# A four-layer graph network: message pass without bias matmuls, two gathered supers done last, sorted part ended earlier

## The reference, cut to what matters

```python
def _sage_mean(h, src, dst, Wl, Wr, b):
    agg = segment_sum(h[src], dst)          # over the edges
    cnt = segment_sum(ones, dst)
    return _l2norm(agg / maximum(cnt, 1) @ Wl + b + h @ Wr)
h = relu(batch_norm(_sage_mean(x, src, dst, Wl1, Wr1, b1)))   # 128 wide
out = _l2norm(_sage_mean(h, src, dst, Wl2, Wr2, b2) + x)      # 64 wide
x = _layernorm(x + out)
```

## Time and profile before

| | us |
|---|---|
| median of 3 runs | 8759.73 (8747.03 to 8762.27) |
| profiled execution, its own time | 8745.67 |
| its span, first to last instruction | 8743.7 |

### The profile page before, as it was taken

One profiled execution on the slowest core, in us unless ns is written; L12 is line 12 of the kernel. 1 busy time (PEld: TensorE's weight loads), 2 busy tenths in 40 slices (PEclk: granted clock), 3 DMA queues, 4 the chain that ended last, 5 costly groups with the idle time before them and its releaser, 6 DMA issues. The chain is left out here.

```text
span 8743.7 us, 127149 instructions
## 1 busy us (share of the span) xinstructions
PE 5411.1 (62%) x29370; PEld 4179.4 (48%) x29371; DVE 3367.5 (39%) x7842; ACT 1499.6 (17%) x3432; POOL 6302.1 (72%) x6643
## 2 busy tenths in 40 slices
PE   4456766666666666667788768778877333333333
PEld 3445555555666666655555545444444222222222
DVE  3224444434444444444445434555554111111111
ACT  1111111111111111112222212233333100000000
POOL 6777777767777777767777752777766477777777
PEclk6556556557777777767878865888888555555555
DMA  3111111113333333334545424544444111111111
GB/s 79 34 34 35 35 35 34 35 37 100 97 98 97 97 98 97 99 99 110 118 111 118 113 61 128 138 145 137 140 140 117 38 30 30 30 30 30 30 30 29
DMA packets 555851, 676.47 MB, mean 77 GB/s; under 512 B 242261, under 2 KB 358003, under 8 KB 555019
## 3 DMA queue, kind: packets, MB, share of 16 engines
q0 software_dynamic: 212448, 268.01, 15.6%
q1 hardware_dynamic: 201194, 306.89, 11.8%
q10 hardware_dynamic: 141441, 93.34, 3.5%
HBM read 574.09 MB, written 93.56 MB: 76 GB/s over the span
## 5 line engine op out<-in xcount | busy, mean ns | idle before, releaser
L1919 PE MATMUL PAG<-OH,G 128*64 128x96 f32 (+1 forms) x10224 | 1573.8, 337 | 2284.0 <-DMA G<-rel_tab,IDX 984.9
L1919 PEld LDWEIGHTS PAG<-OH,G 128*64 128x64 f32 (+1 forms) x10224 | 1424.7, 204 | 2438.6 <-issue 2415.3
L1919 PE MATMUL PH<-HT 125*128 125x192 bf16 (+4 forms) x10742 | 1991.2, 314 | 303.9 <-DVE HT L1449 92.2
L832 POOL DMA_INDIRECT G<-rel_tab,IDX x1507 | 1421.8, 943 | 546.3 <-issue 459.7
L832 POOL DMA_INDIRECT G<-in_x,SRC x1525 | 1451.6, 952 | 481.9 <-issue 464.6
L832 POOL DMA_INDIRECT G<-far_tab,SRC x1527 | 1442.3, 945 | 485.0 <-issue 465.2
L1919 PEld LDWEIGHTS PH<-HT 125*128 125x128 bf16 (+4 forms) x10742 | 1275.7, 156 | 995.6 <-issue 355.2
L1411 DVE TENSOR_TENSOR AGG<-AGG,PAG 64x96 f32 (+2 forms) x852 | 211.2, 248 | 3169.0 <-PE PAG L1919 3148.1
L832 POOL DMA_INDIRECT G<-g_tab,SRC x1040 | 991.6, 953 | 582.7 <-issue 498.5
L832 POOL DMA_INDIRECT G<-x_tab,SRC x1040 | 994.6, 956 | 334.7 <-issue 315.0
L1919 PE MATMUL PAG<-OH,HT 128*128 128x96 f32 x3126 | 611.0, 376 | 524.5 <-ACT HT L1127 518.0
(11 more groups left out here) (222 smaller groups left out, 4438.9 us busy)
## 6 DMA issues: line engine op xcount, KB each, us to landing
HT<-x_parts SPq DMA_DIRECT2D x160, 468.8 KB
HT<-g_parts SPq DMA_DIRECT2D x160, 468.8 KB
GROWS<-rel_tab SPq DMA_DIRECT2D x4096, 0.2 KB
GROWS<-in_x SPq DMA_DIRECT2D x3584, 0.2 KB
HT<-src_rows SPq DMA_DIRECT2D x320, 160.0 KB
rel_tab<-STG ACTq DMA_DIRECT2D x200, 250.0 KB
GROWS<-far_tab SPq DMA_DIRECT2D x3072, 0.5 KB
GROWS<-rel_tab ACTq DMA_DIRECT2D x3072, 0.2 KB
```

The lines of the kernel that those rows point to most:

```text
L832: pool.indirect_dma_start(out=G[:, h, j, 0:tabs[p].shape[1]], out_offset=None, in_=tabs[p], in_offset=bass.IndirectOffsetOnAxis(ap=numbers ...
L1919: return nc.tensor.matmul(dst, lhsT, rhs, start=start, stop=stop, skip_group_check=True)
```

## The change

Four edits.

1. **Message pass.** The two bias matmuls of a unit are gone. SP loads the bias once, spread over 125 partitions. ACT copies only the first half of the bank and stores it to `g_tab`; DVE adds the bias to the second half out of the bank into `MESSAGES`, and SP stores that to `r_tab`. PE's next unit waits for this addition.
2. **Held supers.** In layers 2 and 3 steps 28 and 29 work on the edges of supers 130 and 131, and steps 130 and 131 on those of 28 and 29 (`super_at`). Unit 7, to which 28 and 29 belong, comes last; unit 34 is free at step 30.
3. **Sorted part.** The batches are spread over steps 0 to 117 in place of 125. PE's last `sum_cells` stand before the sum of step 118, and DVE adds the last window at step 119.
4. **Places.** Layer 3 has four places a step, the fourth behind the second batch.

With this, DVE loads the window starts for two supers at a time, not four, and the check on the input has 9 limits in place of 5.

```diff
+HELD = 28
+HELD_UNIT = 7
+BEAT_SLOTS = {2: 3, 3: 4}
+def super_at(p, s):
+    if p not in CELL_LAYERS:
+        return s
+    early = SUPERS_OF[p] - 2
+    return {HELD: early, HELD + 1: early + 1, early: HELD, early + 1: HELD + 1}.get(s, s)
 def batches_by_step(p):
-        due = min(total, -(-total * (s + 1) // (supers - 6)))
+        due = min(total, -(-total * (s + 1) // (supers - 14)))
 def cell_schedule(p):
         if u < apart:
-            needs[u] = (min(at, supers), windows)
-            free[u] = at if at < supers else supers
+            if u < HELD_UNIT:
+                at = min(at, HELD)
+            elif u == HELD_UNIT:
+                at = supers
+            elif u == apart - 1:
+                at = HELD + 2
+            else:
+                at = min(at, supers - 2)
+            needs[u] = (at, windows)
+            free[u] = at
         else:
-            free[u] = step_of.get(BATCHES * windows, supers) + 1
+            free[u] = step_of.get(BATCHES * windows, LAST_BATCH_AT[p] + 2) + 1
-        for _ in range(3):
+        for _ in range(BEAT_SLOTS[p]):
# SP, messages()
+                sp.dma_start(BIAS[0:HALF, :], sb2.to_broadcast([HALF, D])).then_inc(bias_in, 16)
-                    sp.wait_ge(msg_copied, u + 1)
-                    sp.dma_start(rows_of(g_tab, u), MESSAGES[u % 2][0:HALF, :, 0:D]).then_inc(msg_out[u % 2], 16)
+                    sp.wait_ge(msg_rooted, u + 1)
+                    sp.dma_start(rows_of(r_tab, u), MESSAGES[u % 2][0:HALF, :, D:2 * D]).then_inc(msg_out[u % 2], 16)
# POOL: chunk numbers from t = super_at(p, s)
# ACT, messages()
-                    copy(rows_, MESSAGE_P[u % 2].rearrange("p (a c) -> p a c", a=2)).then_inc(msg_copied, 1)
+                    copy(rows_[:, :, 0:D], MESSAGE_P[u % 2].rearrange("p (a c) -> p a c", a=2)[:, :, 0:D])\
+                        .then_inc(msg_copied, 1)
-                    act.dma_start(rows_of(r_tab, u), rows_[:, :, D:2 * D]).then_inc(msg_out[u % 2], 16)
+                    act.dma_start(rows_of(g_tab, u), rows_[:, :, 0:D]).then_inc(msg_out[u % 2], 16)
# DVE, messages()
+                    if u >= 2:
+                        dve.wait_ge(msg_out[u % 2], 32 * (u // 2))
+                    nc.vector.tensor_tensor(MESSAGES[u % 2][0:HALF, :, D:2 * D],
+                                            MESSAGE_P[u % 2].rearrange("p (a c) -> p a c", a=2)[:, :, D:2 * D],
+                                            BIAS[0:HALF, :].unsqueeze(1).to_broadcast([HALF, 2, D]), ALU.add)\
+                      .then_inc(msg_rooted, 1)
# PE, messages()
-                        mm(bank[:, a * H:(a + 1) * H], POS[:, hot + a * HALF:hot + (a + 1) * HALF], wlr2[:, :], a == 0,
-                           False)
-                        last = mm(bank[:, a * H + D:(a + 1) * H], ONES[0:1, 0:HALF], sb2r, False, a == 1)
+                        last = mm(bank[:, a * H:(a + 1) * H], POS[:, hot + a * HALF:hot + (a + 1) * HALF], wlr2[:, :],
+                                  a == 0, a == 1)
# PE, cell_layer()
+                    if s == LAST_BATCH_AT[p] + 1:
+                        for e in range(pairs - LAG[p], pairs):
+                            sum_cells(e)
+                    for now in by_step[s][3:]:
+                        beats(now)
-                for e in range(pairs - LAG[p], pairs):
-                    sum_cells(e)
```

More of the change, by code:

```diff
@@ L60 @@
 IOTA_READY, SPANS_READY, DIAG_READY = 8, 22, 24
-ROWS_READY, COUNTED_READY, PREP_READY, TABLES_READY = 71, 85, 92, 100
+ROWS_READY, COUNTED_READY, PREP_READY, TABLES_READY = 80, 94, 101, 109
 ROWS_OUT = 5 * 16
@@ L94 @@
 CELL_LAYERS = {2: (132, 35), 3: (132, 35)}
+HELD = 28
+HELD_UNIT = 7
+assert HELD % 2 == 0 and SEGMENTS[0][0] <= HELD_UNIT < SEGMENTS[0][1]
 CELL_SUPERS = SLOTS
@@ L136 @@
 BATCHES_AT = {p: batches_by_step(p) for p in CELL_LAYERS}
+LAST_BATCH_AT = {p: max(s for s, batches in enumerate(at) if batches) for p, at in BATCHES_AT.items()}
 def cell_schedule(p):
@@ L283, in gnn_kernel @@
         REGULAR_I = sb("REGULAR_I", [1, 1], I32)
-        CHECKS = sb("CHECKS", [1, 2, 5])
+        CHECKS = sb("CHECKS", [1, 2, 9])
         DST_TAB = HT[:, N - SORTED * UNITS // 2:N].bitcast(F16).rearrange("p (w u) -> p w u", u=UNITS)
@@ L364, in gnn_kernel @@
         o += 2 * D
+        BIAS = HT[:, o:o + D]
+        o += D
         assert o <= N - SORTED * UNITS // 2
@@ L517, in gnn_kernel @@
         msg_split = sem("msg_split")
+        bias_in, msg_rooted = sem("bias_in"), sem("msg_rooted")
         msg_out = [sem("msg_out0"), sem("msg_out1")]
@@ L711, in some_rows @@
                     if at % AT_ONCE == 0:
-                        starts[:] = row_starts(sp, row_registers, p, SP_SUPERS[p][k] // 2, e)
+                        starts[:] = row_starts(sp, row_registers, p, super_at(p, SP_SUPERS[p][k]) // 2, e)
                     row(sp, p, k % ROW_BUFS, e, starts[at % AT_ONCE])
@@ L820, in _, with gathers @@
         def _(pool):
-            def gathers(p, s, base, by_rows=()):
+            def gathers(p, s, base, by_rows=(), edges_of=None):
                 numbers = IDX3 if p == 4 else SRC
@@ L828, in gathers @@
                     pool.wait_ge(summed, base + s + 1)
-                filled = GROUP - 1 if s in by_rows else filled_chunks(s)
+                t = s if edges_of is None else edges_of(p, s)
+                filled = GROUP - 1 if s in by_rows else filled_chunks(t)
                 for j in range(filled):
-                    c = s * GROUP + j
+                    c = t * GROUP + j
                     pool.indirect_dma_start(
@@ L835, in gathers, with layers @@
                     ).then_inc(gathered[h], 16 * (GROUP - j if j == filled - 1 else 1))
-            def layers(supers, base, rows):
+            def layers(supers, base, rows, edges_of=None):
                 for p in range(LAYERS):
@@ L848, in layers @@
                     for s in range(0 if p else SHARED, supers[p]):
-                        gathers(p, s, base[p], rows[p])
+                        gathers(p, s, base[p], rows[p], edges_of)
             even, even_base = [SUPERS] * LAYERS, [SUPERS * p for p in range(LAYERS)]
@@ L860, in _ @@
             with pool.If(regular > 0):
-                layers(SUPERS_OF, BASE, by_rows)
+                layers(SUPERS_OF, BASE, by_rows, super_at)
             with pool.If(regular < 1):
@@ L1284, in _ @@
             link(nc.vector.tensor_reduce(CHECKS[:, 0, 1:2], HT[0:1, 0:SORT_SUPERS], AX.X, ALU.max))
-            limits = [COLS - 1, 0] + [UNIT * apart - 1 for _, apart in CELL_LAYERS.values()] + [P]
+            limits = [COLS - 1, 0] + [UNIT * (apart - k) - WIN for _, apart in CELL_LAYERS.values() for k in (0, 1)]
+            limits += [UNIT * (HELD_UNIT + 1) - WIN, -UNIT * HELD_UNIT, P]
             for k, (supers, _) in enumerate(CELL_LAYERS.values()):
-                link(nc.vector.tensor_reduce(CHECKS[:, 0, 2 + k:3 + k], SPANS[0:1, 0:supers], AX.X, ALU.max))
+                link(nc.vector.tensor_reduce(CHECKS[:, 0, 2 + 2 * k:3 + 2 * k], FIRST[0:1, 0:supers], AX.X, ALU.max))
+                link(nc.vector.tensor_reduce(CHECKS[:, 0, 3 + 2 * k:4 + 2 * k], FIRST[0:1, 0:supers - 2], AX.X, ALU.max))
+            held = CHECKS[:, 0, 6:8]
+            link(nc.vector.tensor_reduce(held[:, 0:1], FIRST[0:1, HELD:HELD + 2], AX.X, ALU.max))
+            link(nc.vector.tensor_reduce(held[:, 1:2], FIRST[0:1, HELD:HELD + 2], AX.X, ALU.min))
+            link(nc.vector.tensor_scalar_mul(held[:, 1:2], held[:, 1:2], -1.0))
             for k, limit in enumerate(limits):
@@ L1729, in messages @@
             def messages():
+                dve.wait_ge(bias_in, 16)
                 for u in range(UNITS):
@@ L1840, in cell_layer @@
                 for s in range(supers):
-                    if s % SLOTS == 0:
-                        for k, w0 in enumerate(starts_of(dve, registers[s // SLOTS % 2], s)):
-                            starts[s + k] = w0
+                    if s % 2 == 0:
+                        pair = registers[s // SLOTS % 2][s % SLOTS:s % SLOTS + 2]
+                        starts[s], starts[s + 1] = starts_of(dve, pair, super_at(p, s))
                     if s:
@@ L1848, in cell_layer @@
                     if s + 1 < supers:
-                        one_hot((s + 1) % 2, DREL[:, s + 1, :]).then_inc(onehot_ready, 1)
+                        one_hot((s + 1) % 2, DREL[:, super_at(p, s + 1), :]).then_inc(onehot_ready, 1)
                     beats(by_step[s][0])
@@ L1856, in cell_layer @@
                         batch(g, s)
+                    for now in by_step[s][3:]:
+                        beats(now)
                     windows_before = max([0] + [g // BATCHES for at in BATCHES_AT[p][:s + 1] for g in at[-1:]])
-                if windows_before:
-                    dve.wait_ge(window_added, WINDOWS_BEFORE[p] + windows_before)
+                    if s == LAST_BATCH_AT[p] + 2:
+                        add_cells(p, windows - 1, s)
+                    if s >= LAST_BATCH_AT[p] + 2:
```

(3 more changed lines are left out.)

4 lines of the change are left out of this document (2 added, 2 removed).

## The result

The changed kernel takes 8783.44 us in the median (8778.69 to 8796.58), the kernel before 8759.73; the ratio is 1.0035 with a 95% interval of 1.0023 to 1.0046. By the medians it is slower by 24 us, by the ratio, which takes in all runs of both kernels, by some 31 us; I had forecast 10 us less. POOL's timeline says in which stage; rows as in the earlier trace rows.

What follows compares the result with a forecast made beforehand. POOL's gathers bound layer 2, PE's program layer 3, a `g_parts` store loop the message pass, with tails behind; −22 − 3 + 0.5 + 12 + 2 = −10.5 us gave 8749.2 us from the median, range 8708 to 8786.

Steps and rivals of the forecast that it cites:

- Tail of layer 2: Behind layer 2's last gather: 8 beats left instead of 17, two units instead of four; −22 us.
- Message pass: PE loses 200 matmuls, but the untouched store loop keeps 2.60 us a unit for 2.65; −3 us, bounds −54 and +10.
- the loop that I named: Message pass: DVE's split, SP's store, its landing, next split into that `g_parts` buffer; 5.20 us for two units.
- the estimate of 1.5 us a unit: Message pass: stores of 125 partitions on 5 engines, some 220 KB a unit, take at least 1.5 us.
- the −42: Message pass: most the bias edit would give, −42 us or less instead of −54, by the DMA engine rate.
- The three stretches: Layer 3: up to the sum of step 118 +40 us, then to the last gather −9, tail −30.5; together +0.5.
- the bound named there: Layer 3, sum of step 118 to last gather: if remaining units keep PE the bound, it stays 107.7 us (0).
- Four places a step: Layer 3: too little PE work between fold and flip, +8 us, denser `rel_tab` stores +4; +12, bounds −25 and +61.
- C: Layer 3: four places make PE wait for `XS` and `STG` in nearly every unit; +45 not +12, 8782 us; chance 0.22.
- B: Layer 3: PE's added work before step 118 fills waits for `GROWS`; +9 not +40, 8718 us; chance 0.33.
- D: Message pass follows PE because stores land sooner; −28 us instead of −3, 8724 us; chance 0.05.
- Prologue: Before the layers: nine more linked DVE instructions at 0.28 us; +2 us, between 0 and +2.5.

Runs made afterwards that it cites:

- l3_three_places: Changed kernel with three places a step in layer 3 instead of four, all else as changed; 8738.37 us, ratio 0.9979.
- l3_as_before: Changed kernel with layer 3 as before: three places, batches to step 125, supers in order; 8737.39 us, ratio 0.9982.
- l3_flip_5_later: Changed kernel, four places kept, one place left empty ahead of each unit's flip in layer 3; 8772.45 us, ratio 1.0023.

## Why the prediction was wrong

- *Tail of layer 2.* −22 predicted. The pass begins 5221.05 − 5190.2 = 30.8 us behind the last gather, it was 53.4: −22.6. Right.
- *Message pass.* −3 predicted; from its first matmul to the first gather of layer 3 137.45 us (5243.91 to 5381.36) became 132.9 (5221.05 to 5353.94), −4.6. The size was right, the cause wrong: the loop that I named does not hold the period, since it stayed at 2.59 us when that loop had four buffers and DVE's wait in it was gone; the transfers do, with the share of 5 of 16 engines never idle. That the size came right is luck: the loop's 5.20 us held a landing that the full transfers had stretched. The floor of 0.3 stands in the kernel before already. The Trainium skill's rule on the engines stood in the prediction as no more than an upper limit of the gain, and wrongly worked out: the estimate of 1.5 us a unit is below PE's own 1.58 and limits nothing, so the −42 does not follow from the numbers beside it.
- *Layer 3 without the places.* The three stretches +40 − 9 − 30.5 = +0.5. l3_three_places against l3_as_before is this part by itself: 1427.4 − 1396.1 = +31.3 in the stage (+31 predicted for the two first; singly, up to the end of the sum of step 118 1285.4 became 1323.8, +38.4 for +40, and behind it 110.7 became 103.6, −7.1 for −9), 53.7 − 89.7 = −36.0 in the gap, and the ratios 0.9979 and 0.9982 cannot be told apart. Right, within what single executions show. In the changed kernel itself the stretch from the sum of step 118 to the last gather did not shrink (107.8, then 107.5 us), the bound named there.
- *Four places a step.* This step failed: +12 predicted, 45 measured twice (8783.44 − 8738.37 with the other edits, 8804.23 − 8759.49 without). I looked for the missing cover in one place, ahead of the flip, and `XS` indeed came to 33.8 us for my 33. But ACT does the chain and the copies in one order, and the chain, no longer broken by a batch, kept the copies from PE first: +52 us of `HT` up to step 118. I named the engines of the chain and not what is queued behind them on ACT. So the sum of step 118 came 95 us later from the layer's first gather, for the 50 that I gave, and POOL waited 189.9 us for PE, for 125. With ACT's copies first the wait for `HT` is gone by half and the kernel is as slow, so the copies are not the whole of it. What else PE waits for stays open; the runs show that most of the price is idle time of PE, 292 us up to step 118 for 253 with three places.
- *Rivals.* C, put at 0.22, gave 8782, and 8783 came; its price, +45, is met, its place (the beat after the fold, `XS` and `STG`) is not: `STG` is at 0.4 us and `XS` at 33.8, not 70. That its number came is luck. B's filling of the waits for `GROWS` is there, 111.7 to 88.9, but that is 23 us against 52 new ones. D did not happen, though the cut stores show that its gain was to be had.
- *Prologue.* +2 predicted; the last gather of layer 2 ends at 5190.2, and ended at 5190.5. Nothing.

## What to carry to other kernels

Before work is packed into the program of an engine that runs it in order, list what stands behind each of its waits and which engine needs that next: here a chain that hops between two engines held up what stood behind it on ACT, and a wait taken from one of its ends came back at the other. When a stage stays at its pace whatever is removed, look for a floor in the busy share of the DMA engines before looking for a loop. Where the floor belongs to stores over an awkward number of partitions, try to cut each into two: 125 into 120 and 5 was worth 28 us here.

## What was not expected of the hardware

- Stores of 125 partitions kept the DMA share at 0.3 or above through the whole message pass; cut into 120 and 5 they took the pass from 2.59 to 2.06 us a unit on the mean, 28 us of the kernel by the medians (8738.37 to 8710.48) and 24 by the ratios, though three more DMAs a unit are issued.
- Behind the wait of 3.08 us shown above, PE ran 6 us at a granted clock of 0.50, 1.2 GHz, where it had run at 1.00, 2.4 GHz, until the wait, and then was back at 0.99. The 16 matmuls of a sum took 1.53 us ahead of the wait (6425.60) and 2.76 us in that stretch (6434.62).

```profile
6420.00:6428.80 8.80, 8.80 (x64) 5.30 (x62) 4.24 (x11) 3.79 (x12) 5.40 (x7) 1.00 0.46 155
...
6431.90:6438.00 6.10, 5.80 (x25) 4.31 (x26) 4.76 (x11) 0.71 (x2) 4.35 (x6) 0.50 0.43 136
6438.00:6450.00 12.00, 11.02 (x62) 5.46 (x60) 3.96 (x7) 4.90 (x11) 9.10 (x10) 0.99 0.48 131
```

- Over the whole stage this does not add up to a price. With four places in the kernel before, PE was idle 26 us longer in layer 3 (291 to 317) and busy 34 us longer (1075.85 to 1109.60) at 0.81 rather than 0.83, for 37 matmul records more out of 5966. But l3_flip_5_later was idle for 346 us at 0.83 and busy for only 1088.28, and the five kernels with the same program in layer 3 were busy for 1112 to 1143 us in it, at 0.79 to 0.81. The first line is the kernel before with four places, the second l3_flip_5_later.

```profile
5398.00:6825.00 1427.00, 1109.60 (x6003) 654.06 (x6001) 722.17 (x1762) 410.20 (x1048) 981.74 (x1027) 0.81 0.47 131
...
5375.00:6809.00 1434.00, 1088.28 (x6022) 650.34 (x6020) 736.16 (x1806) 412.98 (x1065) 976.98 (x1026) 0.83 0.46 131
```
